# A gated cross-attention kernel: sequence 0's projection, sum and norm moved into the last steps of the attention loop

## The reference

```python
x = x + jnp.tanh(g_xattn[0]) * _L0_xattn_ref(_layernorm(x), ctx_1024, ...)
x = x + jnp.tanh(g_ffn[0]) * _L0_ffn_ref(_layernorm(x), ...)
x = x + jnp.tanh(g_xattn[1]) * _L1_xattn_ref(_layernorm(x), ctx_1024, ...)
x = x + jnp.tanh(g_ffn[1]) * _L1_ffn_ref(_layernorm(x), ...)
```

```
a  = softmax(q k / sqrt(8)) v            # self-attention on _ln(r), per head
x1 = r + a @ W_so + b_so                 # the projection and the sum ("xa")
qc = _ln(x1) @ W_cq + b_cq               # the queries of the cross-attention
x2 = x1 + (softmax(qc kc / sqrt(8)) vc) @ W_co + b_co
x3 = x2 + gelu(_ln(x2) @ W_ff1 + b_ff1) @ W_ff2 + b_ff2
```

## Time and profile before

| | |
|---|---|
| median of 3 runs | 439.46 us (438.65 to 443.79) |
| the profiled execution | 441.79 us, its span 440.0 us |
| TensorE busy in the span | 376.2 us (85%) |
| VectorE | 272.0 us (62%) |
| ScalarE | 203.9 us (46%) |
| GpSimd | 114.9 us (26%) |

### The profile page before, as it was taken

One profiled execution on the slowest core, in us unless ns is written; L12 is line 12 of the kernel. 1 busy time (PEld: TensorE's weight loads), 2 busy tenths in 40 slices (PEclk: granted clock), 3 DMA queues, 4 the chain that ended last, 5 costly groups with the idle time before them and its releaser, 6 DMA issues.

```text
span 440.0 us, 6984 instructions
## 1 busy us (share of the span) xinstructions
PE 376.2 (85%) x2612; PEld 216.7 (49%) x2612; DVE 272.0 (62%) x700; ACT 203.9 (46%) x321; POOL 114.9 (26%) x156
## 2 busy tenths in 40 slices
PE   0899899899897999999998699987872899979980
PEld 0667548794343222332323377554562444658870
DVE  5435782232798589888821678535468947775337
ACT  2321512320414477777696477573724336555310
POOL 2100178752325318011110000010000054562442
PEclk9999689999999599999999889999985899889995
DMA  5599111414076465000000000001999667531142
GB/s 114 162 202 326 45 50 46 132 35 124 7 193 153 103 160 112 1 3 1 3 1 1 0 0 2 1 0 50 378 330 290 193 192 250 156 112 57 27 110 60
DMA packets 35877, 46.03 MB, mean 105 GB/s; under 512 B 4778, under 2 KB 21682, under 8 KB 35844
## 3 DMA queue, kind: packets, MB, share of 16 engines
q1 hardware_dynamic: 33156, 38.57, 31.2%
q0 software_dynamic: 2688, 7.02, 5.7%
HBM read 31.67 MB, written 13.78 MB: 103 GB/s over the span
## 4 chain that ended last, share of the span: by engine, by line
PE 49%; DVE 11%; DMA 8%; ACT 7%; issue 4%; POOL 3%; SPq 1%; DVEq 0%; POOLq 0%; ACTq 0%
PE ps L1694 7%; PE ps L1680 6%; PE ps L1463 6%; PE ps L1655 6%; PE ps L1951 4%; PE ps L1796 3%; PE ps L1663 3%; PE ps L1980 3%; DMA R<-h_d,srow 2%; PE ps L1617 2%; PE ps L1805 2%; PE ps L1603 2%; DVE st L989 1%; ACT R L820 1%; PE ps L1901 1%
## 5 line engine op out<-in xcount | busy, mean ns | idle before, releaser
L1272 DVE TENSOR_REDUCE early<-ps 128x1 f32<-128x512 f32 x128 | 81.7, 685 | 14.6 <-PE ps L1655 11.3
L782 ACT ACTIVATE R<-ps 128x1024 f32<-128x1024 f32 x64 | 62.7, 1020 | 24.3 <-PE ps L1680 23.4
L1680 PE MATMUL ps<-R 75*128 75x512 bf16 x128 | 39.8, 399 | 2.3 <-DMA R<-R 2.0
L1655 PE MATMUL ps<-R 72*128 72x512 bf16 x112 | 39.9, 400 | 0.8 <-DVE early L1272 0.8
L1463 PE MATMUL ps<-ident,R 128*77 128x128 f32 (+1 forms) x216 | 33.0, 287 | 6.4 <-DMA R<-disp_d 1.9
L1463 PEld LDWEIGHTS ps<-ident,R 128*77 128x77 f32 (+1 forms) x216 | 24.7, 148 | 25.3 <-issue 7.9
L635 POOL DMA_INDIRECT R<-h_d,srow x16 | 16.5, 1032 | 75.7 <-DMA h_d<-ff 68.6
L1694 PE MATMUL ps<-R,vaug 128*9 128x512 f32 x256 | 34.3, 609 | 0.6 <-ACT R L782 0.6
L1655 PEld LDWEIGHTS ps<-R 72*128 72x128 bf16 x112 | 11.3, 101 | 32.8 <-DVE early L1272 19.2
L552 POOL DMA_INDIRECT disp_d<-R,srow x16 | 16.2, 1015 | 37.3 <-DVE srow L1170 32.7
L1279 DVE RECIPROCAL rden<-ps 128x16 f32<-128x16 f32 x16 | 4.1, 257 | 27.9 <-PE ps L1463 27.7
(11 more groups left out here) (337 smaller groups left out, 742.2 us busy)
## 6 DMA issues: line engine op xcount, KB each, us to landing
R<-in_L_ffn_W_dram SPq DMA_DIRECT2D x1, 6144.0 KB, 19.7
h_d<-R SPq DMA_DIRECT2D x12, 256.0 KB, 4.0
q_d<-R SPq DMA_DIRECT2D x24, 96.0 KB, 1.9
R<-k_d SPq DMA_DIRECT2D x24, 96.0 KB
R<-q_d SPq DMA_DIRECT2D x8, 288.0 KB
R<-in_L_ffn_w_dram SPq DMA_DIRECT2D x1, 2048.0 KB, 16.9
h_d<-ff SPq DMA_DIRECT2D x6, 256.0 KB, 2.6
disp_d<-R SPq DMA_DIRECT2D x1, 1032.0 KB, 11.9
```

The costliest lines, as they stand in the source:

```text
L782: s.activation(probs[idx % 4], ps[:, 2 * (idx % 2):2 * (idx % 2) + 2, :].rearrange("p b t -> p (b t)"), ACT.Exp, scale=QK_SCALE).then_inc( ...
L1272: v.tensor_reduce(mcol[:, u, col:col + 1], bank(ring_bank("row", n)), AX.X, ALU.max).then_inc(s1_max, 1)
L1655: m.matmul(bank(ring_bank("row", n)), Q9[0:KQ, b, h, t * P:(t + 1) * P], K9[0:KQ, b, h, :], start=True, stop=True).then_inc(s1_mm, 1)
L1680: ins = m.matmul(bank(2 * (idx % 2) + j), K9[0:KM, b, h, kt * P:(kt + 1) * P], Q9[0:KM, b, h, :], start=True, stop=True)
```

## The change

The change moves sequence 0's part of that work into the loop. At step 27 (`ATTN0_STEP`) TensorE transposes sequence 0's attention into a ring bank, and VectorE, not ScalarE, copies it; at step 28 TensorE projects it into the next ring bank, and VectorE adds and takes the statistics. The square root of sequence 0 stands on ScalarE behind the last exponentials and ahead of the last output copy. Behind the loop the order is new: VectorE scales sequence 0's tiles before it normalises the last unit; TensorE transposes them ahead of sequence 1's attention, and projects sequence 1 behind sequence 0's query matmul. Cross units start once sequence 0's queries are there. Sequence 1's scaling stands ahead of unit 1's reduction, its transposes behind unit 0's and its query matmul behind unit 1's on TensorE, with the copies beside them on ScalarE; the pass that adds a bias to `xres` (L1318 before) moves ahead of unit 4. Bank numbers become arguments (`at`).

```diff
+ATTN0_STEP = 27
...
+            if st == ATTN0_STEP:
+                ring_order.append(("attn", 0))
+            if st == ATTN0_STEP + 1:
+                ring_order.append(("sum", 0))
...
+                if st == TB * UNITS:
+                    std_of(3, 1, [0])
                 if st >= 4 and st % 4 == 0:
                     evac_oT(st // 4 - 1, pv_mm, st)
...
-            evac_attnT(0, 0)
-            evac_attnT(0, 1)
-            std_of(3, 1, [0])
-
             evac_xT(3, V_LN2, [0])
+            evac_attnT(0, 1, 6)
+            evac_qcT(0, 2)
             std_of(3, 1, [1])
-            evac_qcT(0)
-            evac_xT(3, V_LN2, [1])
-            evac_qcT(1)
...
+                if un == 0:
+                    evac_xT(3, V_LN2, [1], 6)
+                elif un == 1:
+                    evac_qcT(1, 7)
...
+                if st == ATTN0_STEP:
+                    dve.wait_ge(attn_tp, 1)
+                    v.tensor_copy(attnT[:, 0:SEQ], bank(ring_bank("attn", 0))).then_inc(attnT_ready, 1)
+                elif st == ATTN0_STEP + 1:
+                    add_projection(0, 0, ring_bank("sum", 0))
+                    stats_of_sum(0, 0)
+            scale_of(xa, xn, 3, 0)
             normalize(2 * HG - 1, HG - 1, 1)
-            for b in range(B):
-                add_projection(0, b)
-                stats_of_sum(0, b)
-                scale_of(xa, xn, 3, b)
-            me.step(v.tensor_tensor(xres[:, :, :], xa[:, :, :], bias[:, R_CO:R_CO + 1, :].to_broadcast([P, T, D]), ALU.add))
+            add_projection(0, 1, 7)
+            stats_of_sum(0, 1)
 
             for un in range(2 * T):
+                if un == 1:
+                    scale_of(xa, xn, 3, 1)
+                elif un == 4:
+                    me.step(v.tensor_tensor(xres[:, :, :], xa[:, :, :], bias[:, R_CO:R_CO + 1, :].to_broadcast([P, T, D]), ALU.add))
...
+                if st == ATTN0_STEP:
+                    ring_free("attn", 0)
+                    attn_transposes(0, 0, ring_bank("attn", 0))
+                elif st == ATTN0_STEP + 1:
+                    ring_free("sum", 0)
+                    project(0, W_SO, 0, ring_bank("sum", 0))
                 row_tiles(n + 3, 1)
...
-            attn_transposes(0, 0)
+            pe.wait_ge(xa_ready, 1)
             out_transposes(2 * HG - 1)
-            project(0, W_SO, 0)
-            attn_transposes(0, 1)
-            project(0, W_SO, 1)
-            for b in range(B):
-                transpose_tiles(xn, ln_out, 3 * T, ln_tp, [b])
-                pe.wait_ge(xT_ready, 6 + b + 1)
-                m.matmul(bank(2 + b), wx[:, W_CQ, :], xT[:, b * SEQ:(b + 1) * SEQ], start=True, stop=True).then_inc(qc_mm, 1)
+            transpose_tiles(xn, ln_out, 3 * T, ln_tp, [0])
+            attn_transposes(0, 1, 6)
+            cross_queries(0, 2)
+            project(0, W_SO, 1, 7)
...
-                else:
-                    pe.wait_ge(qc_ready, un + 1)
+                if un % T == 0:
+                    pe.wait_ge(qc_ready, un // T + 1)
...
+                if un == 0:
+                    transpose_tiles(xn, ln_out, 3 * T, ln_tp, [1], 6)
+                elif un == 1:
+                    cross_queries(1, 7)
```

More of the change, by code:

```diff
@@ L652, in _, with evac_xT @@
             s = nc.scalar
-            def evac_xT(i, v, batches=range(B)):
+            def evac_xT(i, v, batches=range(B), at=None):
                 for b in batches:
@@ L658, in evac_xT @@
                     dst = xT[:, b * SEQ:(b + 1) * SEQ]
+                    src = bank(b if at is None else at)
                     if v is None:
-                        s.copy(dst, bank(b)).then_inc(xT_ready, 1)
+                        s.copy(dst, src).then_inc(xT_ready, 1)
                     else:
-                        s.activation(dst, bank(b), ACT.Identity, bias=vcol[:, v + 1:v + 2],
+                        s.activation(dst, src, ACT.Identity, bias=vcol[:, v + 1:v + 2],
                                      scale=vcol[:, v:v + 1]).then_inc(xT_ready, 1)
@@ L826, in _ @@
                 if hg == 0:
[L827 removed]
+                    evac_attnT(1, 0, 0)
             std_of(4, 1, [0])
[L829 removed]
+            evac_attnT(1, 1, 1)
             def gelu(b, f):
@@ L1283, in normalize, with add_projection, stats_of_sum @@
                                 ALU.mult).then_inc(o_norm, 1)
+            def add_projection(i, b, at):
+                dve.wait_ge(proj_mm, 2 * i + b + 1)
+                dve.wait_ge(xres_ready, 1)
+                v.tensor_tensor(xa[:, b * TB:(b + 1) * TB, :].rearrange("p t d -> p (t d)"), bank(at),
+                                xres[:, b * TB:(b + 1) * TB, :].rearrange("p t d -> p (t d)"), ALU.add).then_inc(xa_ready, 1)
+            def stats_of_sum(i, b):
+                dve.wait_ge(xa_ready, 2 * i + b + 1)
+                stats(xa, 3 + i, b)
             for n in range(LEAD):
@@ L1467, in spin, with transpose_tiles @@
                 m.matmul(ps[:, 1, 0:columns], ones_b[:, :], zeros[:, 0:columns // 2].bitcast(BF16), start=True, stop=True)
-            def transpose_tiles(src, ready, first, done, batches=range(B)):
+            def transpose_tiles(src, ready, first, done, batches=range(B), at=None):
                 for b in batches:
@@ L1474, in transpose_tiles @@
                             pe.wait_ge(ready, first + b * TB + s + 1)
-                        ins = tp(ps[:, b, s * P:(s + 1) * P], src[:, b * TB + s, :], P)
+                        ins = tp(ps[:, b if at is None else at, s * P:(s + 1) * P], src[:, b * TB + s, :], P)
                     ins.then_inc(done, 1)
@@ L1644, in ring_free @@
                         pe.wait_ge(max_neg, j + 1)
+                    elif before_it == "attn":
+                        pe.wait_ge(attnT_ready, 1)
+                    elif before_it == "sum":
+                        pe.wait_ge(xa_ready, 1)
                     else:
@@ L1735, in row_tiles, with attn_transposes, project @@
                     score_row_tile(k)
+            def attn_transposes(i, b, at):
+                pe.wait_ge(o_norm, 2 * HG * i + HG * (b + 1))
+                transpose_tiles(attn, None, 0, attn_tp, [b], at)
+            def project(i, w, b, at):
+                pe.wait_ge(attnT_ready, 2 * i + b + 1)
+                for s in range(TB):
+                    ins = m.matmul(ps[:, at, s * D:(s + 1) * D], attnT[:, (b * TB + s) * P:(b * TB + s + 1) * P],
+                                   wx[:, w, :], start=True, stop=True)
+                ins.then_inc(proj_mm, 1)
             pe.wait_ge(ld_ones, 16)
@@ L1758, in _, with cross_queries @@
                     out_transposes(u, ring_bank("out", u))
[L1759 to L1772 removed]
+                if st == ATTN0_STEP:
[4 more added lines that the diff above has]
+                    project(0, W_SO, 0, ring_bank("sum", 0))
+                row_tiles(n + 3, 1)
             pe.wait_ge(s1_max, MU * UNITS)
[L1775 removed]
+            def cross_queries(b, at):
+                pe.wait_ge(xT_ready, 6 + b + 1)
+                m.matmul(bank(at), wx[:, W_CQ, :], xT[:, b * SEQ:(b + 1) * SEQ], start=True, stop=True).then_inc(qc_mm, 1)
+            pe.wait_ge(xa_ready, 1)
             out_transposes(2 * HG - 1)
[L1777 to L1785 removed]
+            transpose_tiles(xn, ln_out, 3 * T, ln_tp, [0])
+            attn_transposes(0, 1, 6)
+            cross_queries(0, 2)
+            project(0, W_SO, 1, 7)
             pe.wait_ge(kbd_ready, 1)
@@ L1833, in _ @@
                 if hg == 1:
-                    project(1, W_CO, 0)
-            attn_transposes(1, 1)
-            project(1, W_CO, 1)
+                    project(1, W_CO, 0, 2)
+            attn_transposes(1, 1, 1)
+            project(1, W_CO, 1, 3)
             pe.wait_ge(ld_ff, 32)
```

31 lines of the change are left out of this document (7 added, 24 removed).

## The result

The changed kernel takes 438.01 us in the median of 20 runs (431.38 to 445.22), the one before 441.04 us in 20 runs beside them (435.9 to 448.34), 3.0 us more. The ratio, 0.989 with a 95% interval of 0.9849 to 0.993, is taken over the fast runs of each kernel alone, those within 1.5% of its fastest. By it 4.9 us are gone, 3.1 to 6.7.

The account below looks back on a forecast made before the run. Before the cross units a relay of short handovers bounds the kernel, then TensorE alone. 5.8 us saved there less 1.1 for the longer loop gives 4.7; from 439.46 that forecasts 434.9 us, range 431.8 to 438.8.

Parts of the forecast that it names:

- Term 1: Loop steps 27 and 28: inserted transposes and projection delay ScalarE's exponentials; loop ends 1.1 us later (0.5 to 1.9).
- Term 2: From the last exponential's end to unit 4's transposes: 22.6 us in the new order against 28.4, 5.8 saved.
- T': End of the loop's last exponential in the changed kernel, forecast at 238.6; later points are counted from it.
- The low clock: TensorE between loop and cross units, 249 to 256: granted clock 0.52, mostly 1.2 instead of 2.4 GHz.
- rival A: Between loop and cross units: low clock absent from timed runs or recurring in new kernel, gain 2.3 us, 437.2; chance 0.27.
- Given back further on: Sign of being wrong: the gain at unit 4 is lost again later, at the low stretch behind 324.
- The rule on the table load: Second table load on ScalarE: a drain of about 1380 ns could take 1.2 us, gain 3.5 instead of 4.7.
- B: From T' + 4 on: clock falls and stays low, gain 1.2 us, or 1.3 slower (440.8); chance 0.07.
- C: Loop and low stretch from 328: insertions cost only 0.5 us, stretch shortens, gain up to 8, 431.5; chance 0.11.
- D: Step 28: copies and additions wait for one another, gain ends near 4 us; chance counted within the forecast's 0.55.

## Why the prediction was right

**Term 1** was 1.1 us and is 1.09. The holes are 0.49 and 0.51, as the row of an event of the same kind had said. That the copy is what hides a part of the projection was only half the account: the insertion a step later shows that TensorE's wait behind the copy is what is used up.

**Term 2** was 22.6 and is 22.2. The points on the way: first reduction forecast at T' + 8.6, found at 8.35; unit 4 at 22.6, found at 22.18. The sum was a little long up to the second query matmul (15.9 forecast, 15.3 found), where the handovers were rounded upward, and a little short in it, 0.9 where it takes 1.12. The path is the one described: through VectorE to the second subtraction, then ScalarE, whose last copy ends at 255.43, 0.06 ahead of the query matmul, then TensorE alone. TensorE's own transposes end there too, so between the second subtraction and this matmul the two engines are equally late.

**The low clock** was the weak place. The working compared 28.4 us measured with the low clock against a new order at the full one. Its only reason was the one that it held against rival A, a denser TensorE; in the first 9 us that is 7.05 busy us of 9.00 now, against 8.21 of 11.5 before. The new order does keep the clock, in all six of its profiles, and the kernel before loses it, in both of its profiles; so the difference holds. That the density is the cause was not tried. But of the 5.14 us between the two (39.25 less 34.11), 2.26 are the clock and 2.88 the order, the longer loop's 1.09 already subtracted. Rival A had the size right (2.4) and was wrong in taking it for an accident of this stretch; without that 2.26 the forecast would have been about half as large. Its other half, a low stretch of the new kernel's own, came in another place and not as a property of this kernel: the feed-forward part of its first profile has one, and so has the second profile of the kernel before.

**Given back further on.** The prediction named this as a sign of being wrong. In the first pair of profiles it happened in full: 174.1 us behind unit 4 before, 180.3 after. In the changed kernel's second profile it is 174.0 (431.9 less 257.9), nothing given back, on a chip where the kernel before was not profiled. So the profiles show the gain up to unit 4 and leave open how much of it arrives; that some does is shown by the whole times alone, 0.989 and 0.9917, both intervals below 1. The first pair sets a long execution of the changed kernel beside a middle one of the kernel before, so it doesn't count against them. That the 4.9 us of the first ratio lie so near to 4.6 is in part luck: the medians of all runs are 3.0 us apart, and the interval goes from 3.1 to 6.7.

**The rule on the table load.** The exponential starts at 250.18, 0.03 us behind the end of its table load at 250.15, and the copy behind the root 0.11 us after the root's start. No drain of 1.38 us, as the Trainium skill's page "ScalarE: Activation LUTs" has it in "What ACT_TABLE_LOAD costs", shows at either, nor ahead of the loads, which start 0.02 us behind the instruction before them (240.17 to 240.19, 248.85 to 248.87); the 1.28 us of the load do.

**B and C** did not come: the clock did not fall between T' and unit 4, and the insertions did bite; the low stretch from 328 on, which C wanted shorter, did not get so, and the router's matmuls take 3.45 us in both first profiles. **D**: the projection found the copy ready, the copy having run 230.23 to 230.92 and the projection starting at 231.97.

What the prediction did not see is that the two halves of the change are worth 2.88 us (at the full clock) only together. Had one half been left out, the same way of working would have forecast 2 to 3 us for the other, and I did expect that of them.

## What to carry to other kernels

Where two independent strands lie one behind the other, shortening one moves the end only if the other goes too; write down the second longest path, the engine's own sum of work included, before pricing a single edit. A stretch of short handovers can cost twice, by its waits and by the clock that TensorE loses in them, as here 2.26 us of 28.41: price the stretch at both levels, and try it with dummy matmuls in the holes, which separates the two. With a scatter of 2% between executions, compare lengths between two fixed instructions in the profiles; they agreed to 0.02 us where whole times differed by 10. Then look at what stands behind the second of them: in the first pair of profiles as much was lost there as had been won, and only the repeated whole times say that some of the gain arrives.

## What the runs showed that I had not expected

The lengths between fixed instructions repeat to 0.02 us over executions and chips when the clock is up (C 26.15 twice, 22.18 twice, 21.70 twice, L 11.93 in five kernels), so the scatter of whole times, 431 to 445 us for one kernel, does not arise in these stretches. The changed kernel's two profiles have spans 10.8 us apart (442.7 and 431.9): 4.4 us of it lie ahead of step 27 (228.24 and 223.79) and 6.3 behind unit 4. Time and clock move together: of the changed kernel's 20 runs the fastest, 431.38 us, has a mean granted clock of 0.954, and the slowest, 445.22 us, one of 0.919. One place of it was seen: over the fourteen profiles of this study, the feed-forward part's first eight matmuls took 3.70 us in ten and 5.70 to 6.43 in four. In the kernel before, dummies that compute nothing made 2.26 us of difference in a stretch of 28.
